# The second feed-forward as one pipelined list, and self attention's projections in 512-column pieces

## Chip, cores and metric

One core of a Trainium2 chip (trn2). The metric is the device time of one execution in microseconds, lower is better: 3791.95 us before, the median of three runs (3789.67 to 3794.15).

## What is computed

Four layers, each a gated attention and a gated feed-forward on x of 2 batches x 1,024 tokens x 256 columns, f32. The change touches the feed-forward of layer 1 and the self attention inside layer 3. Layer 1's feed-forward, cut to its core (`act_quant` by token, `weight_quant` by matrix, a convolution of three taps along the tokens for each of 1,024 hidden channels):

```python
def act_quant(x):
    scale = 127.0 / jnp.clip(jnp.max(jnp.abs(x), axis=-1, keepdims=True), 1e-05)
    return jnp.clip(jnp.round(x * scale), -128, 127) / scale
def weight_quant(w):
    scale = 1.0 / jnp.clip(jnp.mean(jnp.abs(w)), 1e-05)
    return jnp.clip(jnp.round(w * scale), -1, 1) / scale
h = bit_linear(layer_norm(x), w1)          # bit_linear quantises both sides
h = depthwise_conv1d(h.transpose(0, 2, 1), conv_w, conv_b).transpose(0, 2, 1)
h = jax.nn.silu(h)
y = bit_linear(h, w2)
x = x + jnp.tanh(g_ffn[1]) * y
```

Layer 3's self attention has 16 heads of 16 columns over 1,024 tokens: `q, k, v` by projections of the normed x, `softmax(q k^T / 4) v`, and an output projection.

## The kernel before

The program is a row of nine stages (l0x, l0f, l1x, l1f, l2x, l2f, l3x, l3a, l3f), each with its own blocks of code for the five engines, and with a barrier at its end (`end_stage`, L84). PE multiplies, DVE, ACT and POOL do the rest, SP issues the loads. Within a stage an engine runs its instructions in the order of its code and waits on semaphores.

**The second feed-forward (stage l1f, `ffn1`, L2614).** `normed` (L1965, names l1fn_) comes first as a block of its own: for each of four chunks of 512 tokens, statistics, root on ACT, normalising, rounding to whole steps of the token's scale, transposes on PE, a copy to bf16 (`xq`), one chunk after the other through DVE. Then `ffn1` loads w1, w2 (1 MB each) and the taps, sums |w| of both, rounds both to -1, 0, 1 (`w1t`, `w2t`), and makes a row of the tokens' steps by multiplying diagonals with ones. A loop over the two batches follows, in it 8 blocks m of 128 hidden channels by 1,024 tokens:

- PE, L2683: four bf16 matmuls into one of two PSUM buffers
- DVE: scaling into `h` (L2758), first tap with the bias into `y` (L2763), second and third tap (L2765, L2767), and the running maximum `big` of the block before (L2751)
- ACT: silu (L2710), then its magnitude (L2714)

`h` and `y` are single buffers:

```python
for m in range(MH):
    dve.wait_ge(s["hid_ready"], b * MH + m + 1)
    nc.vector.tensor_tensor(h[:, 1:S + 1], psf[m % 2], rowb, ALU.mult).then_inc(s["h_ready"], 1)
    ...
    body.add(nc.vector.tensor_scalar(y[:], h[:, 1:S + 1], conv[:, m, 1:2], conv[:, m, 3:4], ALU.mult, ALU.add))
```

After the 8 blocks PE turns `big` (L2689), DVE reduces it to one maximum a token and takes the inverse, PE spreads the inverse over the partitions (L2693), and DVE rounds the 8 blocks with three operations each (L2791, L2793, L2795), PE following with the second product (L2699, 64 matmuls); the last is added to x on DVE (L2799), and SP stores the batch. Then the second batch does the same.

**Self attention (stage l3a).** `plan_self` (L653) writes a list of events that every engine's code walks. There are 16 units (4 heads, 512 queries) of 8 steps. A step has on PE the scores of 128 keys for 4 heads (L985, into the single buffer `slots`), the product with V of the step before (L1001), and two or three pairs of matmuls in bf16 for the maxima of the next unit (L965), which DVE reduces (L1121); on ACT two exponentials (L1081). The maxima share a ring of three PSUM banks with the projections of later units, the `jobs`: K and Q in pieces of 256 columns, V one tile of tokens at a time (L945, L954), each with an evacuation on ACT (L1071, L1073, L1063).

## Time and profile before

| | |
|---|---|
| three runs | 3789.67 to 3794.15 us, median 3791.95 |
| the profiled execution's own time | 3787.75 us |
| its span, first to last instruction | 3786.0 us |
| busy in the span | PE 3041.7, DVE 1739.2, ACT 1281.1, POOL 1231.3 us |
| stage l1f, first DMA issue to that of the next stage | 1436.64 to 1705.91 us |
| mean granted clock of TensorE | 0.893 |

PE is busy 80% of the span. The span is a chain of stages with different limits, so each stage is read by itself. PEld is TensorE's loading of weights beside its matmuls, SPq an issue by SP's queue. A busy PE may be streaming at one of two clocks, 1.2 GHz (shown as 0.5) and 2.4 GHz (1.0); matmuls overlap in their pipeline, so the distance of two starts tells more than a duration.

### The profile page before, as it was taken

What the parts mean: (1) busy time and instruction counts of PE and PEld (TensorE: products, weight loads), DVE (VectorE), ACT (ScalarE), POOL (GpSimd) and SP (SyncE); (2) the same over time, 40 slices, a digit from 0 to 9 for tenths busy, and PEclk for the clock granted to TensorE, in tenths of its full rate; (3) what the DMA queues carried; (4) which work ended last, traced back from release to release, by engine and by line L of the source; (5) the groups of instructions that cost most, each with busy time, mean ns of one, the idle gap of its engine ahead of it and who ended that gap; (6) DMA issues with size and microseconds to landing.
All of it is one profiled execution on the core that took longest, in us unless ns stands there. A gap on an engine that the chain in (4) does not pass through costs nothing. (4 is left out here: it accounts for less than half of the span.)

```text
span 3786.0 us, 42891 instructions
## 1 busy us (share of the span) xinstructions
PE 3041.7 (80%) x15939; PEld 1686.7 (45%) x15939; DVE 1739.2 (46%) x3286; ACT 1281.1 (34%) x1753; POOL 1231.3 (33%) x930
## 2 busy tenths in 40 slices
PE   7887899999999982227739999926886899986696
PEld 3455344443344431113438888813332233325585
DVE  3535546464546446764511111126663777772001
ACT  3333343434343431114302121113442565561231
POOL 2241366566666570002131111042564210000212
PEclk9988999999999995558859999968998999996898
DMA  2102000000000001001134444330001000001453
GB/s 110 62 13 69 9 5 9 7 7 5 9 5 20 1 6 50 11 9 49 46 119 155 169 180 161 149 106 9 1 12 53 1 1 7 7 1 56 158 194 130
DMA packets 94518, 205.60 MB, mean 54 GB/s; under 512 B 9885, under 2 KB 72274, under 8 KB 81556
## 3 DMA queue, kind: packets, MB, share of 16 engines
q0 software_dynamic: 20352, 122.43, 8.5%
q1 hardware_dynamic: 74004, 80.97, 6.6%
q8 instruction: 106, 1.74, 0.2%
q14 instruction: 56, 0.46, 0.0%
HBM read 162.22 MB, written 41.16 MB: 54 GB/s over the span
## 5 line engine op out<-in xcount | busy, mean ns | idle before, releaser
L1503 POOL TENSOR_TENSOR l1x_added<-l1x_added,l1x_probs 128x1024 f32<-128x1024 f32 x224 | 527.1, 2353 | 266.1 <-ACT l1x_probs L1761 198.9
L1859 DVE TENSOR_REDUCE l1x_tops<-l1x_ring 128x1 f32<-128x512 f32 x512 | 326.9, 685 | 206.2 <-PE l1x_ring L1578 205.8
L1121 DVE TENSOR_REDUCE l3a_halves<-l3a_ring 128x1 f32<-128x512 f32 x512 | 325.1, 684 | 107.8 <-PE l3a_ring L965 105.2
L1761 ACT ACTIVATE l1x_probs<-l1x_slots 128x1024 f32<-128x1024 f32 x256 | 261.8, 1023 | 240.3 <-PE l1x_slots L1618 238.5
L1611 PE MATMUL l1x_slots<-l1x_Q,l1x_K 64*128 64x512 f32 x1152 | 312.5, 620 | 7.4 <-ACT l1x_probs L1759 4.8
L1081 ACT ACTIVATE l3a_probs<-l3a_slots 128x1024 f32<-128x1024 f32 x256 | 248.1, 1021 | 151.9 <-PE l3a_slots L985 151.9
L1633 PE MATMUL l1x_pv<-l1x_probs,l1x_V 128*64 128x512 f32 x1152 | 284.6, 609 | 5.2 <-ACT l1x_probs L1759 5.2
L3134 DVE TENSOR_TENSOR l2f_hh<-l2f_sg,l2f_hid 128x256 f32<-128x256 f32 x184 | 77.5, 421 | 294.9 <-ACT l2f_sg L3032 294.9
L3032 ACT ACTIVATE l2f_sg<-l2f_hid 128x256 f32<-128x256 f32 x184 | 70.5, 383 | 384.5 <-PE l2f_hid L2987 384.5
L2987 PE MATMUL l2f_hid<-l2f_xgT,l2f_gate 128*128 128x256 f32 x736 | 190.8, 382 | 1.1 <-ACT l2f_xgT L3021 1.1
L2987 PE MATMUL l2f_hid<-l2f_xgT,l2f_up 128*128 128x256 f32 x736 | 190.0, 381 | 0.0
L985 PE MATMUL l3a_slots<-l3a_Q,l3a_K 32*128 32x512 f32 x1024 | 149.9, 636 | 23.3 <-ACT l3a_probs L1081 22.5
L2998 PE MATMUL l2f_out<-l2f_down,l2f_hh 128*128 128x256 f32 x736 | 162.7, 379 | 0.0
L1503 POOL TENSOR_TENSOR l3x_added<-l3x_added,l3x_probs 128x1024 f32<-128x1024 f32 x56 | 135.6, 2421 | 78.8 <-ACT l3x_probs L1761 68.7
L2987 PEld LDWEIGHTS l2f_hid<-l2f_xgT,l2f_gate 128*128 128x128 f32 x736 | 140.8, 192 | 20.8 <-issue 1.5
L2987 PEld LDWEIGHTS l2f_hid<-l2f_xgT,l2f_up 128*128 128x128 f32 x736 | 140.7, 191 | 19.5
L2998 PEld LDWEIGHTS l2f_out<-l2f_down,l2f_hh 128*128 128x128 f32 x736 | 138.1, 190 | 17.9
L2924 POOL COPY l2f_row_now<-l2f_expert_row 128x1 uint32 (+1 forms) x23 | 4.2, 183 | 428.3 <-PE l2f_out L2998 360.9
L1633 PEld LDWEIGHTS l1x_pv<-l1x_probs,l1x_V 128*64 128x64 f32 x1152 | 72.0, 136 | 156.7 <-issue 126.4
L1611 PEld LDWEIGHTS l1x_slots<-l1x_Q,l1x_K 64*128 64x128 f32 x1152 | 101.4, 189 | 80.0 <-issue 59.3
L1001 PE MATMUL l3a_pv<-l3a_probs,l3a_V 128*32 128x512 f32 x1024 | 137.0, 607 | 0.0
L1537 PE MATMUL l1x_slots<-l1x_lT,l1x_w 128*128 128x512 f32 x256 | 120.7, 615 | 2.2 <-ACT l1x_lT L1698 1.6
...
## 6 DMA issues: line engine op xcount, KB each, us to landing
...
```

The costliest lines, as they stand in the source:

```text
L985: last = nc.tensor.matmul(slots[:, j, :], K[g % 2][rows, i * P:(i + 1) * P], Q[g % 2][rows, h * CH:(h + 1) * CH], start=True, stop=True, t ...
L1001: last = nc.tensor.matmul(pv[32 * j:32 * j + 32, :], V[:, b, i, col:col + 32], probs[:, n % PROBS, j // 2, j % 2 * CH:j % 2 * CH + CH], st ...
L1081: nc.scalar.activation(probs[:, n % PROBS, pair, :], s2[pair], ACT.Exp).then_inc(s["exp_done"], 1)
L1121: nc.vector.tensor_reduce(halves[:, k % 2, col:col + 1], bank_of(banks[e]), AX.X, ALU.max).then_inc(s["bank_done"], 1)
L1503: ins = nc.gpsimd.tensor_tensor(added[h][:], added[h][:], probs[:, n % PROBS, :, :], ALU.add)
L1537: last = nc.tensor.matmul(out[:, h * HALF:(h + 1) * HALF], wi[:, 0 if kind == "q" else 1, k, :], lT[:, k, b * S + h * HALF:b * S + (h + 1) ...
L1611: nc.tensor.matmul(out[:, e * HALF:(e + 1) * HALF], K[i][d, kt * P:(kt + 1) * P], Q[i][d, h * HALF:(h + 1) * HALF], start=True, stop=False ...
L1633: last = nc.tensor.matmul(pv[64 * e:64 * e + 64, :], V[i][:, kt, 64 * e:64 * e + 64], probs[:, n % PROBS, e, :], start=kt == 0, stop=kt == ...
L1761: ins = nc.scalar.activation(p, s2[m % 2], ACT.Exp)
L1859: ins = nc.vector.tensor_reduce(tops[:, e * NT + t, h:h + 1], bank, AX.X, ALU.max)
L2987: last = nc.tensor.matmul(hid[:, m % HID, j, :], wb[i][weight_names[j]][:, col:col + P], xgT[i][:, k, :], start=k == 0, stop=k == KD - 1)
L2998: last = nc.tensor.matmul(out_ps[i][:, t, :], hh[:, k, t * P:(t + 1) * P], wb[i]["down"][:, k * D:(k + 1) * D], start=k == 0, stop=k == MH ...
```

## The change

`ffn1` is written anew and no longer calls `normed`. A function `plan1` lists the events of all engines; there is no loop in the code and one block in place of two.

- Loads: x in chunks with w1 behind the first, taps and w2 behind the second.
- Chunks 0 and 1 are normalised (statistics on DVE, inverse root on POOL, normalising on ACT) and rounded before the first block, chunks 2 and 3 beside batch 0's blocks; w2 is summed and rounded there too. Whole numbers lose their offset on ACT as they are copied to bf16.
- The token's steps are spread by transposing a broadcast column.
- Two buffers of `h`; everything between PE and ACT goes in halves of 512 tokens. POOL builds for each block and tap a diagonal matrix of 128x128 (24 in all, 3 a block). The convolution is matmuls of these with shifted `h`, in f32: three taps for blocks 0 to 3 and 8, 10, 12, 14 (batch 1's are 8 to 15), two for the others, whose last tap DVE adds in PSUM. ACT takes silu with the bias from PSUM.
- Batch 0's inverse is taken two blocks into batch 1; six of its blocks are rounded beside batch 1's blocks 10 to 15 (two operations on DVE, two on ACT), the other two after them. Batch 0's second product follows the last convolution; batch 1's grows block by block behind its rounding.

In self attention a job of K or Q is 512 columns, of V two tiles.

```diff
@@ plan_self
     for g in range(units // 2 - 1):
         if g:
-            for i in range(4):
-                jobs[2 * g, i] = [("k", g + 1, i * 256, 256)]
             for i in range(2):
-                jobs[2 * g, 4 + i] = [("q", g + 1, i * 256, 256)]
-        for i in range(2):
-            jobs[2 * g + 1, i] = [("q", g + 1, CH + i * 256, 256)]
+                jobs[2 * g, 2 * i] = [("k", g + 1, i * CH, CH)]
+            jobs[2 * g, 4] = [("q", g + 1, 0, CH)]
+        jobs[2 * g + 1, 0] = [("q", g + 1, CH, CH)]
-    for i in range(NT):
-        jobs[(5, 2 + i) if i < 6 else (6, i)] = [("v", 1, i, 1)]
+        jobs[(5, 2 + 2 * i) if i < 3 else (6, i * 2)] = [("v", 1, 2 * i, 2)]
@@ ffn1
+def plan1(hidden):
+    plan = [("stats", 0), ("sum", 0), ("stats", 1), ("weights", 0), ("quant", 0), ("turn", 0), ("step", 0), ("quant", 1), ("turn", 1), ("step", 1)]
+    side = {0: [("sum", 1)], 1: [("stats", 2)], 2: [("weights", 1), ("quant", 2), ("turn", 2), ("step", 2)], 3: [("stats", 3)],
+            4: [("quant", 3), ("turn", 3), ("step", 3)]}
+    for g in range(2 * hidden + 2):
+        if g < 2 * hidden:
+            plan += [("up", g, 0), ("up", g, 1)]
+        if 1 <= g <= 2 * hidden:
+            plan += [("conv", g - 1, 0), ("conv", g - 1, 1)]
+        if g >= 2:
+            plan.append(("max", g - 2))
+        plan += side.get(g, [])
+        if g == hidden + 1:
+            plan.append(("big", 0))
+        if g == hidden + 2:
+            plan += [("inv", 0), ("rows", 0)]
+        if hidden + 3 <= g <= 2 * hidden:
+            plan.append(("round", 0, g - hidden - 3))
+    plan += [("big", 1), ("round", 0, hidden - 2), ("inv", 1), ("rows", 1), ("round", 0, hidden - 1), ("round", 1, 0), ("round", 1, 1), ("out", 0)]
+    plan += [("add", 1, 0), ("add", 1, 1)]
+    for m in range(2, hidden):
+        plan += [("round", 1, m), ("add", 1, m)]
+    plan.append(("end", 1))
+    return plan
...
+                if n == 1:
+                    pool.wait_ge(s["conv_loaded"], 16)
+                    for m in range(MH):
+                        for j in range(3):
+                            pool.tensor_scalar(taps[:, m, j, :], c.ident[:], conv[:, m, j:j + 1], None, ALU.mult).then_inc(s["taps_ready"], 1)
...
+            def widen(g, half):
...
+                if i >= 2:
+                    pe.wait_ge(s["h_ready"], i - 1)
+                at = b * S + half * CH
+                for k in range(KD):
+                    last = nc.tensor.matmul(up[:, half, :], wt[0][:, k, m * P:(m + 1) * P], xq[:, k, at:at + CH], start=k == 0, stop=k == KD - 1)
+                last.then_inc(s["up_psum"], 1)
+            def mix(g, half):
...
+                if i >= 2:
+                    pe.wait_ge(s["silu_done"], i - 1)
+                n = 3 if whole[g] else 2
+                for j in range(n):
+                    last = nc.tensor.matmul(mixed[:, half, :], taps[:, m, j, :], h[g % 2][:, half * CH + j:half * CH + j + CH], start=j == 0, stop=j == n - 1)
+                last.then_inc(s["conv_psum"], 1)
...
+            def silu(g, half):
...
+                nc.scalar.activation(act_out[g % KEEP][:, half * CH:(half + 1) * CH], mixed[:, half, :], ACT.Silu, bias=conv[:, g % MH, 3:4]).then_inc(s["silu_done"], 1)
+            def floor(b, m):
...
+                nc.scalar.activation(a[:], a[:], ACT.Relu, bias=whole_part[:, 1:2]).then_inc(s["floored"], 1)
+                act.wait_ge(s["floored"], n + 1)
+                nc.scalar.activation(hq[:, b, m, :], a[:], ACT.Identity, bias=whole_part[:, 2:3]).then_inc(s["hq_ready"], 1)
...
+            def rounded(b, m):
...
+                round_step.add(nc.vector.tensor_tensor(a[:], a[:], inverse_rows[b][:].rearrange("p a n -> p (a n)"), ALU.mult))
+                round_step.wait()
+                nc.vector.tensor_scalar(a[:], a[:], ROUND, ROUND + 127.0, ALU.add, ALU.min).then_inc(s["shifted"], 1)
```

How the order of instructions moves. DVE in the loop over blocks, before (l1f_ps is the product of x and w1, l1f_row the tokens' steps, l1f_mag the magnitude, L50 a helper's register):

```order
L2758 TENSOR_TENSOR l1f_h<-l1f_ps,l1f_row 128x1024
L2751 TENSOR_TENSOR l1f_big<-l1f_mag,l1f_big 128x1024
L2763 TENSOR_SCALAR l1f_y<-l1f_h,l1f_conv 128x1024
L50 REGISTER_ALU
L2765 SCALAR_TENSOR_TENSOR l1f_y<-l1f_h,l1f_conv,l1f_y 128x1024
L50 REGISTER_ALU
L2767 SCALAR_TENSOR_TENSOR l1f_y<-l1f_h,l1f_conv,l1f_y 128x1024
```

And of the change, two steps of batch 1 (l1f_up is the product of x and w1, l1f_mixed the convolution in PSUM, L3027 and L3029 the rounding of a block of batch 0):

```order
L2986 TENSOR_TENSOR l1f_h<-l1f_up,l1f_row 128x512 x2
L3019 TENSOR_TENSOR l1f_big<-l1f_big,l1f_mag 128x1024
L3027 TENSOR_TENSOR l1f_act_out<-l1f_act_out,l1f_rows 128x1024
L3029 TENSOR_SCALAR l1f_act_out<-l1f_act_out 128x1024
L2986 TENSOR_TENSOR l1f_h<-l1f_up,l1f_row 128x512 x2
L2995 SCALAR_TENSOR_TENSOR l1f_mixed<-l1f_h,l1f_conv,l1f_mixed 128x512 x2
L3019 TENSOR_TENSOR l1f_big<-l1f_big,l1f_mag 128x1024
L3027 TENSOR_TENSOR l1f_act_out<-l1f_act_out,l1f_rows 128x1024
L3029 TENSOR_SCALAR l1f_act_out<-l1f_act_out 128x1024
```

Of the taps DVE keeps one in every second block, and a block of batch 0 is rounded in each step.

PE at the passage from batch 0 to batch 1, of the change (L2774 the product of x and w1, L2787 the taps, L2797 turns the maxima of batch 0, L2807 its inverses):

```order
L2774 MATMUL l1f_up<-l1f_xq,l1f_w1t 128x512 x4
L2787 MATMUL l1f_mixed<-l1f_h,l1f_taps 128x512 x6
L2797 MATMUL l1f_misc<-ident,l1f_big 128x128 x8
L2774 MATMUL l1f_up<-l1f_xq,l1f_w1t 128x512 x4
L2787 MATMUL l1f_mixed<-l1f_h,l1f_taps 128x512 x4
L2807 MATMUL l1f_rows<-ident,l1f_inv 128x128 x8
L2774 MATMUL l1f_up<-l1f_xq,l1f_w1t 128x512 x4
L2787 MATMUL l1f_mixed<-l1f_h,l1f_taps 128x512 x6
```

The matmuls of a block's taps stand behind the next block's first product, and the two turns for rounding stand in between. Each of these f32 matmuls is two instructions in the profile.

PE in self attention, two steps of unit 2 before (l3a_ring are the three banks, l3a_slots the scores):

```order
L965 MATMUL l3a_ring<-l3a_Kb,l3a_Qb 128x512 x2
L945 MATMUL l3a_ring<-l3a_xT,l3a_wk 128x256 x2
L965 MATMUL l3a_ring<-l3a_Kb,l3a_Qb 128x512 x2
L985 MATMUL l3a_slots<-l3a_Q,l3a_K 128x512 x4
L965 MATMUL l3a_ring<-l3a_Kb,l3a_Qb 128x512 x2
L1001 MATMUL l3a_pv<-l3a_probs,l3a_V 32x512 x4
L965 MATMUL l3a_ring<-l3a_Kb,l3a_Qb 128x512 x2
L945 MATMUL l3a_ring<-l3a_xT,l3a_wk 128x256 x2
L985 MATMUL l3a_slots<-l3a_Q,l3a_K 128x512 x4
```

and now:

```order
L962 MATMUL l3a_ring<-l3a_Kb,l3a_Qb 128x512 x2
L942 MATMUL l3a_ring<-l3a_xT,l3a_wk 128x512 x2
L962 MATMUL l3a_ring<-l3a_Kb,l3a_Qb 128x512 x2
L982 MATMUL l3a_slots<-l3a_Q,l3a_K 128x512 x4
L962 MATMUL l3a_ring<-l3a_Kb,l3a_Qb 128x512 x2
L998 MATMUL l3a_pv<-l3a_probs,l3a_V 32x512 x4
L962 MATMUL l3a_ring<-l3a_Kb,l3a_Qb 128x512 x2
L982 MATMUL l3a_slots<-l3a_Q,l3a_K 128x512 x4
```

The first step's piece is twice as wide and the second step has none.

## Rows read from the trace of the kernel before

**Rows 1.** The page, 40 slices: granted clock of TensorE, in tenths of 2.4 GHz.

```profile
PEclk9988999999999995558859999968998999996898
```

**Rows 2.** Stage l1f: busy us (x instructions) of PE, PEld, DVE, ACT, POOL; clock.

```profile
1436.60:1705.90 269.30, 75.38 (x306) 44.11 (x306) 194.88 (x297) 45.15 (x48) 0.00 (x0) 0.56 0.07 24
```

**Rows 3.** Groups of instructions: busy us, mean ns | idle before; the last by tile, min/median/max.

```profile
L2767 DVE SCALAR_TENSOR_TENSOR l1f_y<-l1f_h,l1f_conv,l1f_y 128x1024 f32<-128x1024 f32 x16 | 20.6, 1285 | 0.6
L2758 DVE TENSOR_TENSOR l1f_h<-l1f_ps,l1f_row 128x1024 f32<-128x1024 f32 x16 | 19.6, 1226 | 2.0 <-DVE l1f_big L2743 0.5
L2751 DVE TENSOR_TENSOR l1f_big<-l1f_mag,l1f_big 128x1024 f32<-128x1024 f32 x16 | 19.6, 1226 | 18.9 <-ACT l1f_mag L2714 18.9
L2791 DVE TENSOR_TENSOR l1f_act_out<-l1f_act_out,l1f_ps 128x1024 f32<-128x1024 f32 x16 | 19.4, 1215 | 6.6 <-PE l1f_ps L2693 6.6
...
L2714 ACT ACTIVATE l1f_mag<-l1f_act_out 128x1024 f32<-128x1024 f32 x16 | 16.9, 1056 | 0.5
...
L2793 DVE TENSOR_SCALAR l1f_act_out<-l1f_act_out 128x1024 f32<-128x1024 f32 x16 | 11.1, 693 | 0.5
...
L1135 DVE SCALAR_TENSOR_TENSOR l3a_Q<-l3a_ring,l3a_Q x16: 691/692/692, 2945.0 to 3395.8; 128x512 f32<-128x512 f32 x16
```

**Rows 4.** Timeline of one step of the loop: start, us, engine, line.

```profile
1510.89 1.23 DVE L2758 TENSOR_TENSOR l1f_h<-l1f_ps,l1f_row 128x1024 f32<-128x1024 f32 x1
...
1512.18 1.89 PE L2683 MATMUL l1f_ps<-l1f_xq,l1f_w1t 128*128 x4 [5.24 <-DVE l1f_h L2758]
...
1517.86 1.23 DVE L2758 TENSOR_TENSOR l1f_h<-l1f_ps,l1f_row 128x1024 f32<-128x1024 f32 x1
```

**Rows 5.** Timeline of the stage's start, its end, and the next stage's first issue.

```profile
1436.64 2.03 SPq L2007 DMA_DIRECT2D l1fn_x<-x  x4
1440.60 1.41 DVE L2022 BATCH_NORM_STATS2 l1fn_stats<-l1fn_x 128x6 f32<-128x256 f32 x4 [8.22 <-DMA l1fn_x<-x]
1444.42 1.22 DVE L2074 TENSOR_REDUCE l1fn_size<-l1fn_xn 128x4 f32<-128x1024 f32 x1
1448.27 0.69 DVE L2088 TENSOR_SCALAR l1fn_xn<-l1fn_xn 128x1024 f32<-128x1024 f32 x1
1482.03 2.29 DVE L2724 TENSOR_REDUCE l1f_part<-l1f_w 128x1 f32<-128x2048 f32 x1 [0.66 <-DMA l1f_w<-in_l_w]
...
1687.33 9.29 PE L2699 MATMUL l1f_out_ps<-l1f_w2t,l1f_hq 128*128 128x256 bf16 x57 [2.19 <-DVE l1f_hq L2795]
1696.77 3.23 DVE L2799 SCALAR_TENSOR_TENSOR l1fn_x<-l1f_out_ps,l1f_back,l1fn_x 128x256 f32 x8 [9.50 <-PE l1f_out_ps L2699]
1705.91 0.39 SPq L324 DMA_DIRECT2D l2x_x<-x  x1
```

**Rows 6.** First feed-forward, DVE and POOL: by tile (ns min/median/max), and one timeline row.

```profile
L2273 POOL TENSOR_SCALAR l0f_w1l<-l0f_w1l,l0f_gam x2: 598/832/1067, 191.8 to 196.0; 128x128 f32<-128x128 f32 x2
L2493 DVE CUSTOM_DVE_ANT_0 l0f_work<-l0f_xn,l0f_tok x16: 416/422/2579, 187.3 to 216.7; 128x256 f32<-128x256 f32 x16
211.35 10.14 POOL L2292 TENSOR_TENSOR l0f_x<-l0f_x,l0f_b2l 128x1024 f32<-128x1024 f32 x4
```

**Rows 7.** Timeline of PE in the first feed-forward: f32 matmuls of 512 columns.

```profile
199.44 3.78 PE L2341 MATMUL l0f_hid<-l0f_xT,l0f_w1l 128*128 128x512 f32 x4 [10.26 <-POOL l0f_w1h L2274]
210.68 3.60 PE L2341 MATMUL l0f_hid<-l0f_xT,l0f_w1h 128*128 128x512 f32 x8
```

**Rows 8.** Timeline of PE in self attention: first scores of units 12 to 15, and a piece.

```profile
3312.46 1.14 PE L985 MATMUL l3a_slots<-l3a_Q,l3a_K 32*128 32x512 f32 x8 [0.49 <-ACT l3a_probs L1081]
3342.93 1.14 PE L985 MATMUL l3a_slots<-l3a_Q,l3a_K 32*128 32x512 f32 x8 [0.50 <-ACT l3a_probs L1081]
3370.74 1.14 PE L985 MATMUL l3a_slots<-l3a_Q,l3a_K 32*128 32x512 f32 x8 [0.49 <-ACT l3a_probs L1081]
3397.17 1.14 PE L985 MATMUL l3a_slots<-l3a_Q,l3a_K 32*128 32x512 f32 x8 [0.50 <-ACT l3a_probs L1081]
3315.19 1.13 PE L945 MATMUL l3a_ring<-l3a_xT,l3a_wk 128*128 128x256 f32 x4
```

More of the change, by code:

```diff
@@ L2620, in ffn1, with tapped @@
     MH = DH // P
+    G = B * MH
+    KEEP = MH + 4
+    plan = plan1(MH)
+    whole = [g < MH // 2 or g >= MH and g % 2 == 0 for g in range(G)]
+    def tapped(g):
+        return 2 * whole[:g].count(False)
     with ExitStack() as ctx:
@@ L2695, in _ @@
[L2695 removed]
+                    if t >= 2:
+                        pe.wait_ge(s["x_added"], t - 1)
                     for k in range(MH):
[L2697 to L2700 removed]
+                        last = narrow(b, t, k)
@@ new lines, in _ @@
+            for e in plan:
+                if e[0] == "sum":
+                    total(e[1])
+                elif e[0] == "turn":
+                    turn_x(e[1])
+                elif e[0] == "step":
+                    turn_steps(e[1])
+                elif e[0] == "up":
+                    widen(*e[1:])
+                elif e[0] == "conv":
+                    mix(*e[1:])
+                elif e[0] == "big":
+                    turn_big(e[1])
+                elif e[0] == "rows":
+                    turn_inverse(e[1])
+                elif e[0] == "out":
+                    out_tiles(e[1])
+                elif e[0] == "add":
+                    add_up(*e[1:])
@@ new lines, in add_out @@
+            def add_out(b):
+                inv_step.wait()
+                for t in range(NT):
+                    dve.wait_ge(s["out_psum"], b * NT + t + 1)
+                    tile = x[:, b * NT + t, :]
+                    nc.vector.scalar_tensor_tensor(tile, out_of(b, t), back[:, b, t:t + 1], tile, ALU.mult, ALU.add).then_inc(s["x_added"], 1)
+            for e in plan:
+                if e[0] == "stats":
+                    norm(e[1])
+                elif e[0] == "quant":
+                    quantise(e[1])
+                elif e[0] == "sum":
+                    add_weights(e[1])
+                elif e[0] == "weights":
+                    ternary(e[1])
+                elif e[0] == "up":
+                    spread(*e[1:])
+                elif e[0] == "conv":
+                    last_tap(*e[1:])
+                elif e[0] == "max":
+                    largest(e[1])
+                elif e[0] == "inv":
+                    inverse(e[1])
+                elif e[0] == "round":
+                    rounded(*e[1:])
+                elif e[0] in ("out", "end"):
+                    add_out(e[1])
```

424 lines of the change are left out of this document (272 added, 152 removed).

## The prediction

> **What bounds the kernel now.** I read the forty slices first, then the stage's totals, its groups of instructions, its timeline, and for prices the timelines of stages that already do such work. The slices [rows 1] show TensorE's clock at half (a 5 is the level of 1.2 GHz) for longest in slices 16 to 18, nearly all of which is the second feed-forward. The totals [rows 2] say what it waits for there: in 269.3 us PE is busy 75.4, ACT 45.2, POOL 0, DVE 194.9. DVE is the bound, and what it doesn't fill is the chain between it and the others. The groups [rows 3] give one step of the loop over 16 blocks (8 of each batch): the scaling out of PSUM L2758 1.23 us, the maximum L2751 1.23, two taps of 1.28 (L2767 and its like), the first tap, and 18.9/16 = 1.2 us of waiting for ACT's magnitude. Steps stand 1517.86 - 1510.89 = 6.97 us apart [rows 4]. So 16 steps are 112 us; normalising, weights and scaling rows take the first 61, and rounding with the second product, alone after each loop, the rest. The stage runs from 1436.64 to 1705.91 [rows 5]. Nothing of another stage overlaps it (each ends in a barrier), so what it loses or gains the kernel does.
>
> **The change, part by part.** I lay the new stage end to end, counted from 1436.64.
>
> *Start, to the first tap matmul: 32.6 us.* The first chunk of x is there at +4.0 [rows 5]; its statistics take 1.8; the sum of |w1| 2.3 (L2724; w1 has twice the bytes of that chunk and is issued right behind it, so I take +7 for its landing, an estimate, and the sum ends at +9.3). Statistics of chunk 1: 11.1. Ternary w1, two passes over 2,048 columns, about 1.25 each (twice L2793's 0.69 over 1,024 [rows 3] less what is fixed in it), and small ones: 14.0. Rounding a chunk ran from 1444.42 to 1448.97 with one pass of 0.69 more than now: 4.0 each, two of them: 22.0. Then transposes, ACT's copies, two up products at half clock and the first scaling: about 6.6, so 28.6. To this I add 4 us for POOL. It now builds 24 diagonal matrices (128x128) while DVE rounds. Two such POOL operations took 0.60 and 1.07 us (L2273) [rows 6], and DVE's L2493 on 128x256, 0.42 at the median, took 2.58 at its longest, which is the length of POOL's L2292 beside it (10.14/4 = 2.54). So DVE waits whole POOL operations out. Bounds: 0 (they interleave in gaps) and 24 x 0.83 = 20; I take 4, nearer to 0, since only part of DVE's operations meet one, and each of those meets a short one. The Trainium skill, SBUF — State Buffer, "Who interferes with whom", speaks against this part: VectorE and GpSimd share a port pair under an exclusive lock, and the loser blocks fully. By that rule alone the upper bound would be due, and the stage 16 us longer; the trace agrees in the one place named.
>
> *Batch 0's eight steps: 51.0.* An f32 matmul of 128x512 is two instructions 0.43 us apart at full clock (8 took 3.60, with the pipeline's end) and 0.86 at half (4 took 3.78) [rows 7]. A tap on both halves of a block is thus 4 instructions, 1.72 us; three taps 5.16, two 3.44. The up product in bf16 is 4 matmuls, 1.89 at half clock [rows 4], 0.86 at full. PE per step: 6.0 with three taps, 4.3 with two. The list gives three to blocks 0 to 3, 8, 10, 12, 14, so either batch holds 4 of each: 41.3. DVE per step: scaling 2 x 0.69 (a half block from PSUM, L1135 [rows 3]), maximum 1.23, with two taps 1.4 more: 2.6 or 4.0, under PE. Its side work in this batch is 16.5 us, of which only step 2 (ternary w2 and a chunk, 6.8, besides 2.6) goes over PE's 6.0: 2.5 as a stall. Transposes and rows of chunks 2 and 3: 3.2. The half clock in the first taps and after the stall: 4 (between 0 and 10).
>
> *Batch 1's eight steps: 47.5.* Again 41.3 on PE. DVE now also rounds a block of batch 0 in six of them, 1.21 + 0.69 [rows 3]: 4.5 and 5.9, a pair 10.4 against PE's 10.3; ACT has 2 x 0.7 silu, 1.06 magnitude (L2714) [rows 3] and two passes for rounding, 4.5. With three engines this close, and silu standing behind the rounding on ACT, I take 10.7 a pair, so 42.8. Turning maxima and inverses 2.1, and 2.6 in which PE stands before the inverse of batch 0 (last tap 0.7, reduction and small steps 1.9).
>
> *Tail: 47.4.* From the last convolution: tap, silu, magnitude, maximum 4.0; transposes 2; one rounding beside, then the inverse 1.9; its transposes 2 (to 9.9). Rounding of batch 0's last block reaches PE at 12.4; 64 matmuls of the second product, which went at 9.29/57 = 0.163 [rows 5], take near 9.5 and DVE adds the last tile at 22.6. DVE stands here, since six of batch 1's eight roundings come after these adds in its list. Six roundings on ACT (2.15 each, ACT the slower) end at 37.4; the last 22 matmuls and adds 4.1; store and barrier 5.9, as now from the end of the last addition, 1700.00, to 1705.91.
>
> Sum 32.6 + 51.0 + 47.5 + 47.4 = 178.5 against 269.3: 90.8 us less.
>
> *Self attention.* 58 projection pieces of 256 columns become 29 of 512. A unit of 8 steps with six pieces took 3342.93 - 3312.46 = 30.47, one with none 3397.17 - 3370.74 = 26.43 [rows 8]: 0.67 a piece, though its 4 matmuls keep PE near 1.1 (L945) [rows 8]; 0.4 hides in PE's wait. A 512 piece needs 4 x 0.43 = 1.72 and about 0.2 besides, as the short one does, less the same 0.4: 1.5 against 2 x 0.67 = 1.34. But after a long piece DVE has caught up, and PE's waits for its reductions behind the pieces go. Net -1 us; bounds: 29 x 0.3 = +9 if the long piece only holds up the scores, and -9 if a bank less taken is worth as much. ACT's evacuations, half as many, lie beside PE's scores, as now.
>
> So 92 us less: the profiled execution's 3787.75 (span 3786.0) becomes 3695.8. It lies 4.2 below the median of the three runs, 3791.95, so **3700** for the median.
>
> **Rivals.**
> *A, the list stalls more than I count*: rounding, silu and taps wait for each other in turn, each of batch 1's steps costs 7.0 as now rather than 5.35 (+13), POOL's diagonals cost 14 instead of 4 (+10). Stage 202, kernel 3723. For it: every buffer between PE and ACT is one half deep. Against: PE's order puts an up product before each convolution.
> *B, it overlaps better*: the start at 26, steps at PE's own pace, a tail of 42 since rounding goes faster: 163, kernel 3685.
> *C, the clock stays at half through the taps*, as it does now in 0.56 of full on average [rows 2]: 68.8 us of taps double, 247, kernel 3769. For it: PE fell to half in this very stage. Against: PE then waited 5 us in each 7; in the first feed-forward such matmuls, at half clock at 199.44, ran at full clock by 210.68 [rows 7]. The Trainium skill, TensorE: Matmul & The Clock Gate, "HAM oscillation", would have stalls put the clock back each time; by it the kernel would lie between 3700 and 3769.
> *D, slower than before*: the ring of waits closes. PE's up product waits for scaling, taps for scaling and silu, silu for the last tap, all through single buffers; if each waits for the one before, PE is thin, and the half clock follows. Then a step is 1.7 + 1.4 + 10.3 (6.9 with two taps) + 1.4 + 1.3, about 14.4 on average; 16 of them 230, with start and tail 310: kernel 3832. It decides where a step exceeds 11.8 us. Against: two buffers of h and an up product issued a block ahead break the ring; I see no place where it closes.
> *E, the change doesn't do what it says*: if the list kept rounding of batch 0 out of batch 1 (it doesn't, by the order), 16 us more: 3716, within A.
>
> **How the numbers follow.** The forecast as summed 0.60, A 0.18, B 0.12, C 0.07, D 0.03. Terms between their bounds (start -3 to +10, clock -4 to +6, batch 1 -3 to +13, tail -5 to +5, self attention -9 to +9) seldom fall together. From B's side to a little beyond A's, 3678 to 3728 leaves out C, D and the corners, under 2 in 10. About 0.2% is what a measurement of this kernel tells from no change. Every case but D is faster by more: 0.96, the same 0.01, slower 0.03.
>
> **What would show it.** In the changed profile: the stage 178 us long; the loops at 5 to 6 us a step with PE's clock near 1.0; tap matmuls 0.43 apart; DVE no longer the busiest engine in them; POOL's 24 diagonals in the start with DVE's operations beside them lengthened; a wait of PE for the inverse of batch 0; DVE waiting for the second product in the tail; units of self attention within 1 us of now. A stage over 205, a clock near 0.5 in the loops, or self attention off by 5 us would make me wrong in that step.

## The result

The changed kernel takes 3687.22 us, the median of 4 runs (3684.95 to 3691.89), where the kernel before took 3791.71 (4 runs, 3789.67 to 3794.15): a ratio of 0.973, 95% interval 0.9718 to 0.9741. 3700 was forecast, range 3678 to 3728. The profiled execution took 3691.89 us, span 3690.2, and the one of before 3787.75, span 3786.0.

The profile's slices: PE's granted clock no longer lies at half for slices 16 to 18 [rows 1], where it now reads 6, 9, 6; what is low there is the stage's start (ahead of the loops), its tail and the next stage's start.

```profile
PE 3085.5 (84%) x15969; PEld 1694.9 (46%) x15969; DVE 1663.8 (45%) x3193; ACT 1323.9 (36%) x1787; POOL 1254.3 (34%) x978
...
PEclk9998899999999996969579999868998999995898
```

The stage from its first issue to the next stage's, as the timeline of SP has them:

```profile
1430.62 0.36 SPq L2692 DMA_DIRECT2D l1f_x<-x  x1
...
1604.38 0.36 SPq L324 DMA_DIRECT2D l2x_x<-x  x1
```

173.76 us, against 269.27 [rows 5]: 95.5 less, where 90.8 less was forecast. The next view cuts it where the prediction cut it: start, batch 0's eight blocks (first tap matmul to batch 1's first), batch 1's (to the end of its last tap matmul), tail. Columns: from:to and length, busy us (x instructions) of PE, PEld, DVE, ACT, POOL, granted clock, DMA share, GB/s.

```profile
1430.62:1461.26 30.64, 9.52 (x36) 6.95 (x37) 20.32 (x45) 11.01 (x16) 20.30 (x40) 0.56 0.41 137
1461.26:1511.67 50.41, 46.37 (x137) 21.54 (x136) 34.27 (x69) 26.89 (x37) 3.39 (x8) 0.96 0.00 0
1511.67:1557.26 45.59, 42.28 (x121) 18.78 (x119) 33.02 (x45) 29.19 (x34) 0.00 (x0) 1.00 0.00 1
1557.26:1604.38 47.12, 25.40 (x145) 17.67 (x144) 32.49 (x47) 26.89 (x26) 0.00 (x1) 0.68 0.13 45
```

Where [rows 2] had DVE busy 194.9 of 269.3 us and PE 75.4, PE is now busy 88.7 of 96.0 us in the two loops, at a clock of 0.96 and 1.00, and DVE 67.3. Only the loops are full of PE's work: start and tail, 78 us, hold 35 us of it.

Where the 95.5 us come from shows when the stage of before is cut at the like places: the first product of a block, the turn of batch 0's maxima, the first scaling of batch 1, the turn of its maxima.

```profile
1497.83 4.48 PE L2683 MATMUL l1f_ps<-l1f_xq,l1f_w1t 128*128 x12 [4.39 <-ACT l1f_row L2706]
...
1556.15 1.97 PE L2689 MATMUL l1f_ps<-ident,l1f_big 128*128 128x128 f32 x8 [21.17 <-DVEq L2770]
...
1600.43 1.23 DVE L2758 TENSOR_TENSOR l1f_h<-l1f_ps,l1f_row 128x1024 f32<-128x1024 f32 x1 [0.25 <-DVE l1f_big L2743]
...
1657.39 1.97 PE L2689 MATMUL l1f_ps<-ident,l1f_big 128*128 128x128 f32 x8 [21.17 <-DVEq L2770]
```

That gives 61.2 us of start, 58.3 and 57.0 for the two loops, and 44.3 and 48.5 for rounding and second product behind each. Now the start is half as long (30.6 less), the two loops together 19.3 less though they also hold chunks 2 and 3, w2 and five of batch 0's roundings, batch 0's 44.3 no longer stand by themselves, and the tail is only 1.4 less than the 48.5. So most of the gain is work that no longer stands alone; the faster step of the loops is a fifth of it.

The stage's groups (busy us, mean ns | idle before and its releasers); they stand against [rows 3]:

```profile
L2787 PE MATMUL l1f_mixed<-l1f_h,l1f_taps 128*128 128x512 f32 x160 | 73.6, 607 | 0.7 <-ACT l1f_act_out L2894 0.7
...
L2894 ACT ACTIVATE l1f_act_out<-l1f_mixed,l1f_conv 128x512 f32<-128x512 f32 x32 | 21.7, 683 | 40.1 <-PE l1f_mixed L2787 27.3 <-DVE l1f_mixed L2995 12.9
L2986 DVE TENSOR_TENSOR l1f_h<-l1f_up,l1f_row 128x512 f32<-128x512 f32 x32 | 20.7, 687 | 22.6 <-PE l1f_up L2774 22.6
...
L2906 ACT ACTIVATE l1f_act_out<-l1f_act_out,l1f_whole_part 128x1024 f32<-128x1024 f32 x16 | 18.2, 1139 | 13.4 <-DVE l1f_act_out L3029 13.4
L3019 DVE TENSOR_TENSOR l1f_big<-l1f_big,l1f_mag 128x1024 f32<-128x1024 f32 x14 | 17.0, 1218 | 0.1
```

The tap matmuls (L2787) wait 0.7 us in all. DVE's scaling (L2986) waits 22.6 for PE; its maximum (L3019) waits 0.1, where the one of before waited 18.9 for ACT's magnitude. In the loops the bound has passed from DVE to PE. A view of PE's timeline in the start and at the third block shows where PE still stands:

```profile
1454.63 1.39 PE L2774 MATMUL l1f_up<-l1f_xq,l1f_w1t 128*128 128x512 bf16 x4
1459.16 0.59 PE L2743 MATMUL l1f_rows<-l1f_part,ones 128*128 128x1 f32 x2 [3.13 <-DVE l1f_part L2962]
1459.60 1.87 PE L2774 MATMUL l1f_up<-l1f_xq,l1f_w1t 128*128 128x512 bf16 x4
1461.26 7.37 PE L2787 MATMUL l1f_mixed<-l1f_h,l1f_taps 128*128 128x512 f32 x12
...
1477.02 1.10 PE L2751 MATMUL l1f_misc<-ident,l1f_xn 128*128 128x128 f32 x8 [2.37 <-DVE l1f_xn L2958]
```

Self attention went from 553.06 to 551.35 us. The rest of the difference between the two profiles is other stages, which the change leaves alone: the first cross attention 172.06 to 166.12, the next stage (l2x) 160.78 to 164.82, layer 2's feed-forward 654.04 to 656.44. In the 13 profiles taken after the change l0x lay between 166.1 and 172.1, l2x between 157.2 and 165.1, l3f between 340.1 and 345.1, while the second feed-forward of an unchanged kernel came out at 173.76, 173.77 and 173.77. Layer 2's feed-forward lay between 656.4 and 657.5 in all 13, above the one profile of before; why is open. So experiments below are read by the stage, and the kernel's time stands beside it. The two stages account for 97 of the 104 us between the medians; the other 7 are of the size of that scatter, and with one profile of before I can't place them.

### The profile page after: what moved, and what is told of

Same layout as the page of the kernel before. It is cut to its first block and busy times, and to the rows that moved or that the text cites. A ratio compares the mean times of both kernels' runs of the same rounds, so it can differ in the third digit from the quotient of the medians.

```text
span 3690.2 us, 42790 instructions
## 1 busy us (share of the span) xinstructions
PE 3085.5 (84%) x15969; PEld 1694.9 (46%) x15969; DVE 1663.8 (45%) x3193; ACT 1323.9 (36%) x1787; POOL 1254.3 (34%) x978
## 5 line engine op out<-in xcount | busy, mean ns | idle before, releaser
L982 PE MATMUL l3a_slots<-l3a_Q,l3a_K 32*128 32x512 f32 x1024 | 150.0, 636 | 35.3 <-ACT l3a_probs L1078 34.4
## 6 DMA issues: line engine op xcount, KB each, us to landing
slots_in<-zeros POOLq DMA_DIRECT2D x1, 5888.0 KB, 26.8
```

Source lines behind the costliest of these rows:

```text
L982: last = nc.tensor.matmul(slots[:, j, :], K[g % 2][rows, i * P:(i + 1) * P], Q[g % 2][rows, h * CH:(h + 1) * CH], start=True, stop=True, t ...
```

## The experiments

The table has the stage's four parts in every kernel (us), cut as above. The kernels ran in groups on different chips, where the median of the kernel before was 3789.4 to 3792.0, so differences of 2 or 3 us in the last column say nothing, and a single run says less.

| kernel | start | batch 0 | batch 1 | tail | stage | kernel, us (runs) |
|---|---|---|---|---|---|---|
| changed | 30.6 | 50.4 | 45.6 | 47.1 | 173.8 | 3687.2 (4) |
| changed, again | 30.7 | 50.4 | 45.6 | 47.1 | 173.8 | 3685.4 (5) |
| self attention's old pieces | 30.7 | 50.4 | 45.6 | 47.1 | 173.8 | 3691.6 (5) |
| taps all on PE | 30.7 | 57.3 | 48.3 | 45.6 | 181.8 | 3690.9 (5) |
| two taps on PE everywhere | 29.6 | 58.7 | 47.7 | 47.5 | 183.5 | 3702.5 (5) |
| rounding after the loop | 29.8 | 50.6 | 44.3 | 61.9 | 186.6 | 3699.3 (5) |
| diagonals on ScalarE | 30.2 | 64.3 | 45.6 | 47.0 | 187.1 | 3705.7 (1) |
| sum of w2 later | 26.8 | 50.2 | 45.6 | 47.6 | 170.1 | 3685.0 (1) |
| additions spread in the tail | 29.8 | 50.6 | 45.6 | 43.9 | 169.9 | 3681.4 (1) |
| sum later, filler products | 26.0 | 48.5 | 45.6 | 46.9 | 167.0 | 3679.6 (1) |
| the same, ternary w2 later | 25.9 | 47.7 | 48.4 | 47.7 | 169.7 | 3684.0 (1) |
| everything | 25.9 | 47.7 | 48.4 | 42.7 | 164.7 | 3679.5 (5) |
| everything, ternary w2 back | 26.0 | 48.5 | 45.6 | 39.1 | 159.1 | 3677.1 (5) |

The start has a scatter of its own. Numbers 4 and 7 leave its order of instructions as it is, yet it came out at 29.8, since PE's clock had risen by the second chunk's transposes, where it had not in the changed kernel; the half clock then came back at the third block. Start and batch 0 together took 80.4 in these two and 81.1 in the three profiles of the changed stage, so effects under 1 us there are read from rows, not from the table.

**1. Self attention's old pieces** in the otherwise changed kernel:

```diff
-                jobs[2 * g, 2 * i] = [("k", g + 1, i * CH, CH)]
-            jobs[2 * g, 4] = [("q", g + 1, 0, CH)]
-        jobs[2 * g + 1, 0] = [("q", g + 1, CH, CH)]
+            for i in range(4):
+                jobs[2 * g, i] = [("k", g + 1, i * 256, 256)]
...
-        jobs[(5, 2 + 2 * i) if i < 3 else (6, i * 2)] = [("v", 1, 2 * i, 2)]
+    for i in range(NT):
+        jobs[(5, 2 + i) if i < 6 else (6, i)] = [("v", 1, i, 1)]
```

> The changed kernel with self attention's projections in pieces of 256 columns again; the second feed-forward stays new. The prediction's working (two short pieces cost 1.34 us where a long one costs about 1.5 less the waits it covers, net -1 for the change): self attention, 551.4 us in the changed profile, becomes 552 to 553, the kernel stays within 0.1% of the changed one (+1 us). Rival, a long piece only holds up the scores (29 x 0.3): -9 us, stage near 542. Rival, a PSUM bank less taken was worth as much as the working's other bound: +9 us, stage near 560.

Self attention took 553.59 us: 2.2 longer than in the changed kernel, a little above the 552 to 553 expected. It was 553.06 in the kernel before and 550.2 to 551.7 in all twelve profiles with the long pieces. The kernel's median is 4.4 us longer; what goes beyond the stage's 2.2 is within the scatter of the other stages. Units of eight steps with three long pieces stand 30.18 us apart, with six short ones 30.46 (30.47 in [rows 8]), and one without pieces takes 26.42 and 26.43. So a long piece costs (30.18 - 26.42)/3 = 1.25 us and two short ones 1.34. Three groups of PE in that stage, first of the changed kernel:

```profile
L982 PE MATMUL l3a_slots<-l3a_Q,l3a_K 32*128 32x512 f32 x1024 | 150.0, 636 | 35.3 <-ACT l3a_probs L1078 34.4 <-DVE l3a_Q L1132 0.8
...
L962 PE MATMUL l3a_ring<-l3a_Kb,l3a_Qb 32*128 32x512 bf16 x512 | 99.6, 381 | 16.4 <-DVE l3a_halves L1118 16.4
...
L942 PE MATMUL l3a_ring<-l3a_xT,l3a_wk 128*128 128x512 f32 x48 | 23.8, 618 | 0.8
```

then with the old pieces:

```profile
L985 PE MATMUL l3a_slots<-l3a_Q,l3a_K 32*128 32x512 f32 x1024 | 149.9, 635 | 23.3 <-ACT l3a_probs L1081 22.5 <-DVE l3a_Q L1135 0.8
...
L965 PE MATMUL l3a_ring<-l3a_Kb,l3a_Qb 32*128 32x512 bf16 x512 | 99.6, 381 | 21.1 <-DVE l3a_halves L1121 21.1
...
L945 PE MATMUL l3a_ring<-l3a_xT,l3a_wk 128*128 128x256 f32 x96 | 27.1, 405 | 1.6
```

PE's busy time falls by 7.3 us (478.7 to 471.4), and its waits for the maxima by 4.7, as predicted; but 11.9 us more go into waiting for the exponentials (22.5 to 34.4). What is left, with some 2 us less in gaps too short to be given a releaser and at the stage's end, is 2.2 us. Both bounds of 9 us are out.

**2. Three taps on PE everywhere**, and **3. two taps everywhere**, one line each (number 3 has `[False] * G`):

```diff
-    whole = [g < MH // 2 or g >= MH and g % 2 == 0 for g in range(G)]
+    whole = [True] * G
```

> All 16 blocks take their three taps on TensorE (the changed kernel: blocks 0 to 3, 8, 10, 12, 14). A tap of a block is 4 instructions of 0.43 us, 1.72 us. Theory that TensorE bounds both loops: batch 0 +6.9 (4 blocks more), batch 1 +6.9, kernel +13.8 us. Theory of the prediction that three engines are near each other in batch 1 while TensorE alone bounds batch 0: batch 0 +6.9, batch 1 less, +3 to +5, because the last tap of the two-tap blocks (0.75 on VectorE, twice) and the wait for it before silu go; kernel +10 to +12. Rival, waits for VectorE's last tap hold the loops: batch 1 unchanged or shorter, kernel +7 or less.

Batch 0 +6.9, as both theories had it: PE sets it to the tenth of a microsecond. Batch 1 +2.7, less than the +3 to +5 of the prediction's side. PE has 6.9 us more of taps there too, but they fill its own waits: the 2.62 us ahead of batch 0's inverse and the 0.7 us ahead of block 15's taps are gone. The tail is 1.5 shorter, which neither had (no last tap stands ahead of the last silu). Stage +8.1. Part of the kernel's smaller +3.6 is that l2x happened to take 157.2 in that profile.

> All 16 blocks take two taps on TensorE and the last on VectorE. Theory that TensorE bounds both loops: 8 x 1.72 = 13.8 us less, the stage 160. Theory of the prediction: batch 0 is bound by TensorE but for its side work, so -4 to -6 there; in batch 1 a block costs VectorE 2 x 0.69 + 1.22 + 2 x 0.75 + 1.21 + 0.69 = 6.0 where a pair now takes 10.7 (5.35 a block), so VectorE becomes the bound in the six blocks with rounding beside them and batch 1 grows by 2 to 4; kernel -1 to -4 us. Rival, single PSUM halves between the engines: each two-tap block waits out convolution, tap and silu in turn, and both loops get longer, kernel +5 or more.

The rival has the sign, and the kernel is 15 us longer, but none of the three has the place. With 8 x 1.72 = 13.8 us of taps less on PE the stage is 9.7 us longer, and it is batch 0 that grew, by 8.3, by waits for the side work. The timeline of PE there:

```profile
1479.89 1.97 PE L2751 MATMUL l1f_misc<-ident,l1f_xn 128*128 128x128 f32 x8 [7.41 <-DVE l1f_xn L2958]
...
1500.27 1.97 PE L2751 MATMUL l1f_misc<-ident,l1f_xn 128*128 128x128 f32 x8 [7.39 <-DVE l1f_xn L2958]
1502.03 1.06 PE L2761 MATMUL l1f_rows<-ident,l1f_step_size 128*128 128x128 f32 x4
1502.88 1.91 PE L2774 MATMUL l1f_up<-l1f_xq,l1f_w1t 128*128 128x512 bf16 x4
1504.59 4.42 PE L2787 MATMUL l1f_mixed<-l1f_h,l1f_taps 128*128 128x512 f32 x8
```

PE stands 7.4 us twice for chunks 2 and 3, which DVE rounds in the third and fifth step behind the last taps it now also has; the waits were 2.37 and 1.67. And what PE does next runs at half clock (8 transposes in 1.97 against 1.10). The three taps of blocks 0 to 3 are thus not spare work: they keep DVE free for its side work, and PE busy while it does it. In batch 1 VectorE's bound appeared as I had said (+2.1): from block 10's last tap on it worked without a stop, 5.5 us a block, where 6.0 had been summed.

**4. Rounding of batch 0 behind the loop of batch 1**

```diff
-            plan.append(("round", 0, g - hidden - 3))
-    plan += [("big", 1), ("round", 0, hidden - 2), ("inv", 1), ("rows", 1), ("round", 0, hidden - 1), ("round", 1, 0), ("round", 1, 1), ("out", 0)]
+    plan += [("big", 1), ("inv", 1), ("rows", 1)] + [("round", 0, m) for m in range(hidden)] + [ ("round", 1, 0), ("round", 1, 1), ("out", 0)]
...
-    KEEP = MH + 4
+    KEEP = 2 * MH
```

> Batch 0's eight blocks are rounded only after batch 1's loop and inverse (with a buffer for each block of both batches, so that nothing waits for them). Theory that rounding beside batch 1 is what the pipelined list earns there: six of eight blocks at ScalarE's 2.29 us (1.14 + 1.15) go behind the loop, +13.7 us, while the loop of batch 1 returns to TensorE's pace, 45.6 down to about 43 with the wait of 2.6 for the inverse still there, so the kernel +10 to +13 us (the prediction's case E has +16). Rival, ScalarE and VectorE hold batch 1's loop up by about what they round in it: kernel +3 us or less.

```profile
1512.83:1557.10 44.27, 41.55 (x119) 19.02 (x119) 24.06 (x35) 19.46 (x24) 0.00 (x0) 1.00 0.00 1
1557.10:1619.00 61.90, 25.28 (x144) 17.30 (x144) 41.66 (x57) 36.96 (x34) 0.00 (x0) 0.65 0.10 34
```

The loop gives back 1.3 us (to 44.3, not 43), the tail takes 14.8 more: +12.8 in the stage, +12 in the kernel. The first theory holds. In the loop 9.7 us of ACT's work and 9.0 of DVE's are taken away and PE's pace doesn't notice but for 1.3. The rounding beside batch 1 is hidden almost whole, and it is 13 of the stage's 95.

**5. Diagonals on ScalarE**, to measure what POOL's 24 cost DVE in the start:

```diff
-                            pool.tensor_scalar(taps[:, m, j, :], c.ident[:], conv[:, m, j:j + 1], None, ALU.mult).then_inc(s["taps_ready"], 1)
...
+            def diagonals(m):
+                if m == 0:
+                    act.wait_ge(s["conv_loaded"], 16)
+                for j in range(3):
+                    nc.scalar.activation(taps[:, m, j, :], c.ident[:], ACT.Copy, scale=conv[:, m, j:j + 1]).then_inc(s["taps_ready"], 1)
```

with `diagonals(0)` behind the rounding of w1 and `diagonals(m + 1)` behind the magnitude of block m of batch 0.

> GpSimd builds no diagonal matrices; ScalarE builds three behind rounding w1 and three more behind each block's magnitude in batch 0. What it tells is the price of GpSimd's 24 operations beside VectorE in the start. The prediction's term (+4): the distance from the stage's start to the first tap matmul, 30.6 us, shrinks by 4, the stage from 173.8 to about 170. The full lock between the two (VectorE stands for every GpSimd operation beside it, 15 us of them): shrinks by 10 or more. The reading of the changed trace (VectorE's rounding passes 1.34 beside GpSimd against 1.14 alone, small ones 0.23 and 0.30 against 0.17): 0.7 us or less.

The start became 0.5 us shorter (30.64 to 30.15). Rows of the changed kernel with POOL beside, then of this one without:

```profile
1444.47 15.16 POOL L2731 TENSOR_SCALAR l1f_taps<-ident,l1f_conv 128x128 f32<-128x128 f32 x24
...
1445.77 1.34 DVE L2956 TENSOR_SCALAR l1f_xn<-l1f_xn,l1f_scale 128x256 f32<-128x256 f32 x4
```

```profile
1449.12 1.14 DVE L2961 TENSOR_SCALAR l1f_xn<-l1f_xn,l1f_scale 128x256 f32<-128x256 f32 x4
```

The start alone would prove little, since it moves by 0.9 without an edit, but here the transposes ran at half clock in both, and DVE's last rounding pass ends 0.6 us earlier after the stage's start. So 0.5 to 0.6 is the price, not 4 and not 10. But the stage is 13.3 longer, which no theory had: PE waits in the steps of batch 0, from the sixth block on in this way.

```profile
1507.87 3.67 PE L2782 MATMUL l1f_mixed<-l1f_h,l1f_taps 128*128 128x512 f32 x8 [2.72 <-DVE l1f_h L2991]
```

```profile
1505.11 0.69 ACT L2895 ACTIVATE l1f_act_out<-l1f_mixed,l1f_conv 128x512 f32<-128x512 f32 x1 [1.03 <-DVE l1f_mixed L3000]
1505.83 1.06 ACT L2902 ACTIVATE l1f_mag<-l1f_act_out 128x1024 f32<-128x1024 f32 x1
1506.80 0.97 ACT L2885 ACTIVATE l1f_taps<-ident,l1f_conv 128x128 f32<-128x128 f32 x3
```

The row names DVE as the releaser, but ACT's diagonals end at 1507.77 and PE starts at 1507.87: the next block's taps stand behind this block's silu and magnitude, 0.69 + 1.06 + 0.97 = 2.72. That is a flaw of my edit (they belong one block earlier), not of the idea.

**6. The sum of |w2| a step later**

```diff
-    side = {0: [("sum", 1)], 1: [("stats", 2)], 2: [("weights", 1), ("quant", 2), ("turn", 2), ("step", 2)], 3: [("stats", 3)],
+    side = {1: [("sum", 1), ("stats", 2)], 2: [("weights", 1), ("quant", 2), ("turn", 2), ("step", 2)], 3: [("stats", 3)],
```

> The sum of |w2| (2.3 us on VectorE, and TensorE's tiny product behind it) moves one step down the list, behind the first block's convolution. Theory: TensorE's wait of 3.13 us for that sum ahead of its second up product is a loss of the new order, and the sum fits into the 5.2 us in which VectorE now waits at 1463.9 to 1469.1: first tap 3 us earlier, the stage 3 us shorter (170.7). Rival: VectorE is what sets the first three steps (its side work), the sum only moves, and the stall ahead of the third block's transposes grows from 2.4 to 5.4 us: stage unchanged.

The start is 3.9 us shorter: 3.1 of it are the wait, 0.7 the second up product, which went faster (1.20 us for 1.87) as the clock hadn't fallen ahead of it. The first taps run at full clock too (12 in 5.32 us for 7.37), but the half clock comes back behind the third block's transposes and takes 1.7 there, so batch 0 is only 0.2 shorter. The stall ahead of those transposes is 2.37 as before, the stage 3.6 shorter. The first theory holds. The wait was PE's: the tiny product L2743 for the sum is ahead of the second up product in PE's order.

**7. Additions of batch 0 spread through the tail**

```diff
...
+    for m in range(hidden):
+        plan += [("round", 1, m), ("add", 1, m)] + [("tile", 0, t) for t in {0: [0], 1: [1, 2], 2: [3, 4], 3: [5, 6], 4: [7]}.get(m, [])]
...
```

> In the tail VectorE adds batch 0's eight output tiles one or two at a time between batch 1's roundings, instead of all eight before the last six roundings. Theory: ScalarE, which stands 7.1 us there, sets the end; it goes through without that stop, and the tail is 6 to 7 us shorter (stage 167), with the last six roundings still 2.2 us each. Rival: TensorE's second product of batch 0, which has two PSUM banks, waits for the later additions and its end moves back by what is gained: stage shorter by 2 or less.

Half of it came. In the changed kernel ACT stands once, for the additions; here four times, most of it because the first addition stands too early and DVE itself waits for PE. ACT's row before, then ACT's and DVE's rows here:

```profile
1582.24 1.15 ACT L2906 ACTIVATE l1f_act_out<-l1f_act_out,l1f_whole_part 128x1024 f32<-128x1024 f32 x1 [7.08 <-DVE l1f_act_out L3029]
```

```profile
1578.31 1.15 ACT L2905 ACTIVATE l1f_act_out<-l1f_act_out,l1f_whole_part 128x1024 f32<-128x1024 f32 x1 [2.27 <-DVE l1f_act_out L3028]
...
1575.93 0.48 DVE L3034 SCALAR_TENSOR_TENSOR l1f_x<-l1f_misc,l1f_back,l1f_x 128x256 f32<-128x256 f32 x1 [2.62 <-PE l1f_misc L2810]
```

7.08 us of waiting became 3.4, and the tail is 3.2 shorter: ACT sets it, though the 6 to 7 forecast didn't come.

**8. Filler products**, with the sum moved:

```diff
+            def idle_work(n):
+                for _ in range(n):
+                    nc.tensor.matmul(mixed[:, 0, 0:P], c.ones[:], c.ident[:], start=True, stop=True)
```

10 ahead of the first transposes, 2 ahead of the second, 3 ahead of the second block's up product.

> The kernel with the sum of |w2| moved, and 15 more small f32 products (ones by identity, results unused) on TensorE in its waits before the first block: 10 ahead of the first transposes, 2 ahead of the second, 3 ahead of the second block's up product. Theory: the first taps run at half clock (12 in 7.37 us where later 12 take 5.32) because TensorE idled before; kept busy, it is at full clock there, and the stage is 2 to 3 us shorter than with the sum moved alone. Rival: the fillers only delay what stands behind them, and the clock falls in the short waits anyway: 0 to +1 us.

The stage is 3.15 us shorter than with the sum moved alone, but not in the way I gave: with the sum moved the first taps already ran at full clock (12 in 5.32). The gain lies in the start (0.8: the second eight transposes in 1.09 where they took 1.97), in batch 0 (1.7: clock 1.00 against 0.97, since up product and taps after the 2.37 wait stay at full), and 0.7 in the tail, where the edit does nothing. The first of these can't be put down to the fillers: in numbers 3, 4 and 7, without them, the second eight transposes took 1.09 to 1.10 as well. Rows of number 7, then of this one:

```profile
1455.87 1.09 PE L2750 MATMUL l1f_misc<-ident,l1f_xn 128*128 128x128 f32 x8 [1.27 <-DVE l1f_xn L2957]
...
1464.16 5.91 PE L2786 MATMUL l1f_mixed<-l1f_h,l1f_taps 128*128 128x512 f32 x12
...
1478.46 1.48 PE L2750 MATMUL l1f_misc<-ident,l1f_xn 128*128 128x128 f32 x8 [2.37 <-DVE l1f_xn L2957]
```

```profile
1457.49 5.32 PE L2787 MATMUL l1f_mixed<-l1f_h,l1f_taps 128*128 128x512 f32 x12
...
1471.32 1.09 PE L2751 MATMUL l1f_misc<-ident,l1f_xn 128*128 128x128 f32 x8 [2.37 <-DVE l1f_xn L2968]
```

What speaks for the fillers is that all four kernels that have them (numbers 8, 9, 10, 12) ran at full clock from the second transposes to the end of batch 0, and none of the nine profiles without them did. So their worth is near the 1.7 of batch 0; the rest of the 3.15 is not shown to be theirs.

**9. Ternary w2 later**, on top of 8: the entry `("weights", 1)` goes from step 2 to step 8, and only the mean is taken at step 2.

> The kernel with the sum moved and the filler products, and ternary w2 (two passes of 1.25 us on VectorE, one of 2.0 on ScalarE) moved from the third step to the first step of batch 1. Theory: the stall ahead of the third block's transposes (2.37 us) is made by these passes, and the later step, with three taps on TensorE and little on VectorE, has room: batch 0 is 2 to 3 us shorter, batch 1 within 0.5, the stage 167.0 becomes 164 to 165. Rival: VectorE bounds the whole stretch to chunk 3's rounding, so the wait before chunk 3 stays and more waits turn up in batch 1, where VectorE also rounds: 0 to +1 us.

The rival had the sign, but not the size: 2.75 longer, where it had 0 to 1. The stall at the third block fell by 0.8 only, since DVE then stood 1.89 for ACT's normalised chunk; batch 1 grew by 2.9 and the tail by 0.8. Of the 2.9, 1.2 come with a wait of 0.95 for DVE's maximum, the rival's mechanism. The other 1.7 are half clock: the clock fell behind the 2.62 us for the inverse, a wait just as long in number 8, where PE went on at full clock (up product 1.03, taps 5.32).

```profile
1512.80 1.09 PE L2797 MATMUL l1f_misc<-ident,l1f_big 128*128 128x128 f32 x8 [0.95 <-DVE l1f_big L3033]
...
1520.82 1.09 PE L2807 MATMUL l1f_rows<-ident,l1f_inv 128*128 128x128 f32 x8 [2.62 <-DVE l1f_inv L3020]
1521.74 1.70 PE L2774 MATMUL l1f_up<-l1f_xq,l1f_w1t 128*128 128x512 bf16 x4
1523.23 6.38 PE L2787 MATMUL l1f_mixed<-l1f_h,l1f_taps 128*128 128x512 f32 x12
```

**10. All of it.**

> All together: sum of |w2| and ternary w2 later, filler products, batch 0's output additions spread over batch 1's roundings (first one a block later than in the tail run, where VectorE stood 2.62 us for it), and the last block's third rounding pass on VectorE in place of ScalarE's two. If the gains add up: start and batch 0 -9 us (as the runs before), tail -3.2 as in the tail run, -2.3 for its first stop, -2 for the last block: stage 158 to 160, kernel 14 to 16 us below the changed one, near 3673. Rival: the tail is not set by ScalarE alone, TensorE waits for additions: stage 162 or more.

Stage 164.7, where 158 to 160 was forecast; the rival's 162 or more holds, and with it that PE waits for additions: in the tail, 4.3 us shorter than in number 8, PE stands 3.06 us for one. Batch 1 again took 48.4, with the same half clock as in number 9; without that number's loss the stage would have been 162 (by subtraction). The kernel is 6 to 8 us below the changed one, not 14 to 16.

**11. The changed kernel again.**

> The changed kernel once more, for its scatter beside the others of this call: every theory has the second feed-forward at 173.8 us, self attention at 551.4, and the kernel within 0.15% of 3687; the first and third cross attention's neighbours moved by 4 to 6 us between profiles without a change in them, and I expect them to do so again.

3685.38 us (3680.39 to 3690.82), ratio 0.9727, interval 0.9714 to 0.9741. The second feed-forward 173.77, self attention 550.73; l0x 172.05 where it was 166.12, l2x 158.52 where it was 164.82.

**12. The version kept**: sum later, fillers, the additions as below, and the last block's third rounding pass on DVE.

```diff
+        plan += [("round", 1, m), ("add", 1, m)] + [("tile", 0, t) for t in {1: [0], 2: [1, 2], 3: [3, 4], 4: [5, 6], 5: [7]}.get(m, [])]
...
+                if n == G - 1:
+                    dve.wait_ge(s["last_shifted"], 1)
+                    nc.vector.tensor_scalar(hq[:, b, m, :], a[:], ROUND - 128.0, -ROUND, ALU.max, ALU.add).then_inc(s["last_ready"], 1)
```

> As the run with everything together, but ternary w2 back in its old place (moving it had cost 2.75 us: 3.6 lost in batch 1 and the tail, 0.8 won), and batch 0's last output addition one block earlier, since TensorE stood 3.06 us for it. Sum from the runs before: 166.99 (sum moved, fillers), less 4.2 in the tail (46.9 to 42.7), less 2 for the earlier addition: stage 161, kernel about 3675. Rival: TensorE's catching up of batch 1's tiles after the additions is what ends the tail, whatever the additions' order: stage 163.

```profile
1436.19:1462.15 25.96, 12.23 (x64) 10.68 (x66) 17.87 (x44) 11.01 (x16) 17.20 (x35) 0.66 0.48 162
1462.15:1510.63 48.48, 44.34 (x137) 21.02 (x138) 36.73 (x70) 26.91 (x37) 6.50 (x14) 1.00 0.00 1
1510.63:1556.21 45.58, 42.17 (x119) 18.78 (x119) 33.02 (x45) 29.18 (x34) 0.00 (x0) 1.00 0.00 1
1556.21:1595.30 39.09, 20.70 (x145) 16.08 (x144) 32.38 (x48) 25.07 (x24) 0.00 (x1) 0.81 0.16 54
```

159.1, 14.7 less than the changed kernel's stage, 8.0 of it in the tail; 161 was forecast, 163 the rival's. The kernel: 3677.07 us (5 runs, 3670.73 to 3680.59), 0.9698 of before, interval 0.9684 to 0.9711, just below that of number 11. That is 8 to 10 us less than the changed kernel; part of the difference to 14.7 is that layer 0's feed-forward, which the edit leaves alone, took 185.3 in this profile and 182.1 to 182.5 in all others.

## Why the prediction was right, step by step

*Start, 32.6; measured 30.6.* Two errors of opposite sign. POOL's diagonals were put at 4 and cost 0.5 (number 5). The Trainium skill, SBUF — State Buffer, "Who interferes with whom", has the one that comes second block fully; here DVE's four passes took 1.34 for 1.14 while POOL's operations ran beside them, so DVE hardly ever stood for a whole one. The step that failed is "DVE waits whole POOL operations out": it rested on one maximum beside an operation of 2.54 us, and these last 0.60. In the other direction, PE's order was not read closely enough: the sum of |w2| was counted as DVE's side work and not as a wait of PE, and moving it is worth 3.9 (number 6). The remaining terms were 2.3 too long together. That the start came within 2 us is luck: 3.5 and 2.3 too much against 3.9 not seen.

*Batch 0, 51.0; measured 50.4.* PE's 41.3 is right to the tenth: steps of 6.0 and 4.3 as worked out. The stall at the third block was 2.37 (2.5 forecast, but 6.8 + 2.6 - 6.0, the figures it was taken from, is 3.4, so the hit is no proof of them). The one of 1.67 ahead of chunk 3 was not foreseen, and the half clock took 2.1 in the first taps instead of 4; these two nearly cancel. That DVE's side work goes under PE is true only because the first four blocks have three taps (number 3); I had counted DVE against PE step by step, and never asked what the choice of blocks was for.

*Batch 1, 47.5; measured 45.6.* The mis-sized term is "10.7 a pair": blocks 10 and 11 went at PE's own 10.3, blocks 12 and 13 took 10.6. The wait for batch 0's inverse was 2.62, as forecast. Taking ACT's and DVE's rounding away gave 1.3 (number 4), so rivalry of three engines hardly exists there; rival A, with 7.0 a step, is out. Case E had 16 for rounding outside the loop; it is 12.8.

*Tail, 47.4; measured 47.1.* DVE stands for batch 0's second product as described and adds its last tile at 23.1 (22.6 forecast), and ACT stands 7.08 us for DVE meanwhile. That the sum is right to 0.3 is again two errors: the last addition ended at 42.9 (41.5 forecast), and store and barrier took 4.2 instead of 5.9.

*Self attention, -1; measured -1.7 in the profiles, -2.2 by number 1.* A long piece costs 1.25 instead of 1.5; two short ones 1.34, as taken from [rows 8]. The waits for DVE's reductions shrank by 4.7, as said; that nearly all of PE's gain would go into waits for the exponentials was not.

Rival B had the loops' steps at PE's own pace, which came, but not its start of 26 nor its tail of 42; experiments reached both later (26.0 and 39.1). Rival C is out: the clock was 0.96 and 1.00 in the loops. By the Trainium skill, TensorE: Matmul & The Clock Gate, "HAM oscillation", idle gaps between bursts put the clock back; the runs agree for the 7.4 us waits of number 3, while behind 2.37 us it fell in number 6 (12 taps in 5.78) and not in the changed kernel (5.32). Rival D's step of 14.4 is out: the taps wait 0.7 us for silu in the whole stage.

The sum missed by 4.7 us in the stage and 0.7 to 1.2 in self attention. The other 7 of the 12.8 between 3700 and 3687.2 are those that I can't place. The 4.2 added to come from the profiled execution to the median held for before only: there the profiled execution was faster than all four runs, while that of the changed kernel, 3691.89, was the slowest of its four and lies 4.7 above their median.
